# Attention: turning the spread reciprocal weights with TensorE's transpose instruction instead of with products against the identity

## The chip, the cores and the metric

The kernel runs on one core of a Trainium2 chip. The metric is the device time of one execution in microseconds, the median of several runs. Five engines work side by side and wait for each other by semaphores: TensorE (PE; its weight loads are listed apart as PEld), VectorE (DVE), ScalarE (ACT), GpSimd (POOL) and SyncE (SP), which issues most DMA.

## The reference

Four layers on `x` of 4 x 512 x 512 (batch, rows, features), each added to its input:

```python
x = x + top5120_mask(fside * cond * softmax(x) / sqrt(512))   # 1: a mask of ones, diagonal excluded
xn = rms_norm(x) * g_norm * (1 + scale(cond)) + shift(cond)    # 2: attention, 16 heads of 32
q, k, v = heads(xn @ W_qkv); q, k = rms_norm(q)*g_q, rms_norm(k)*g_k
attn = softmax(q @ k.T / sqrt(32)); o = attn @ v
x = x + o + o @ W_out
x = x + gru(x)                                                 # 3: 512 time steps, one after the other
x = x + grid_sample(x, cond)                                   # 4
```

The change concerns the division in the softmax of layer 2: each row of `attn @ v` of a head is divided by the sum of the exponentials of that row.

## The kernel before, in words

The program of every engine is written out by hand, in order, with semaphores between them. The order is: the search for the 5120th value (some 200 us), then the attention of batch 0, 1, 2 and 3 (`pe_attention`, `act_attention`, `dve_attention`), then the 512 recurrent steps (some 1,520 us).

The attention of a batch `b` has two parts. The first projects q, k and v (L1654), stacks and turns q and k (L1673) and, from the second batch on, multiplies the output of the batch before by W_out (L1696). The second runs 32 units, `UNITS`: 4 groups `g` of 4 heads, in each 4 tiles `t` of 128 queries, in each 2 pairs of heads. For unit n:

- PE makes two score tiles of 128 x 512 (`pe_scores`, L1717), two units ahead of the rest (`AHEAD`).
- DVE takes the row maxima of both (`dve_maxima`, L1279); POOL (L515; for batch 3 DVE, L1282) scales and negates them.
- ACT makes the exponentials of the two tiles and their row sums `k.weight` (`act_exponentials`, L750).
- PE transposes them, eight tiles of 128 x 128 in float32 (`pe_turn`, L1733); ACT (L795) and DVE (L1363) copy one half each out of PSUM.
- PE multiplies by v with four heads side by side in the array (`pe_weighted_values`, L1751), one quarter of half a group per unit, four units behind.

Because a group's result is held with features on partitions (`k.oT`, 128 features x 512 queries) but the sums stand with queries on partitions, the reciprocals must be turned. DVE makes the reciprocals of a group's sums (L1371) in the last unit of the group. POOL spreads each over the 32 features of its head into `k.oT[:, g]` (L471): 4 tiles of 128 queries x 128 features. `pe_divide` (L1757 to L1767) turns these four tiles into one PSUM bank: this is the place of the change. ACT copies the bank back over `k.oT[:, g]` (`act_divide`, L757), and DVE multiplies the group's products by it (`dve_divide`, L1290).

In PE's order, `pe_divide` of group g stands at the end of unit 8g + 11 for g below 3, between that unit's values (L1751) and the next unit's scores (L1717); for g = 3 it stands after the last values of the batch and before the transposes and normings for the next batch (`pe_columns`, L1619 and L1630), or in batch 3 before the products with W_out (L1696). There are 16 calls, four tiles each. In ACT's and DVE's order the two steps behind it stand in unit 8g + 12: ACT's copy after the exponentials of unit 8g + 13 and before L795, DVE's product after the maxima of unit 8g + 14 and before L1363. PE waits in `pe_divide` for POOL's spread and for DVE's product of the group before.

Of the kernel before, what the change touches and what calls it, by code (L numbers as in the profile page):

```python
# [16 lines left out]
P = 128  # L17
B, S, D = 4, 512, 512
# [359 lines left out]
VALUES_BANK, DIVIDE_BANK = (6, 7, 6, 7), (7, 6, 7, 6)  # L378
# [1378 lines left out]
def pe_divide(e, k, b, g):  # L1757
    s = k.sem
    n = NC * b + g
    e.wait_ge(s["inv_spread"], n + 1)  # L1760
    if g:
        e.wait_ge(s["out_cols"], n)
    else:
        e.wait_ge(s["heads_dve"], TURNS * (b + 1))
    for t in range(NT):
        made = e.matmul(k.bank(DIVIDE_BANK[g], S)[:, t * P:(t + 1) * P], k.oT[:, g, t * P:(t + 1) * P], k.ident[:], start=True, stop=True)  # L1766
    made.then_inc(s["inv_turned"], 1)  # L1767


def pe_attention(e, k, b):  # L1770
# [26 lines left out]
    for n, (g, t, pair) in enumerate(UNITS):  # L1797
        if n + AHEAD < len(UNITS):
            pe_scores(e, k, b, n + AHEAD)
        pe_turn(e, k, b, n)  # L1800
        if n >= 4:
            group, kt = divmod(n - 4, 4)
            pe_weighted_values(e, k, b, group // 2, group % 2, kt)
            if group % 2 == 1 and kt == NT - 1:
                pe_divide(e, k, b, group // 2)
    for kt in range(NT):
        pe_weighted_values(e, k, b, NC - 1, 1, kt)
    pe_divide(e, k, b, NC - 1)
    if b + 1 < B:
        pe_columns(e, k, b + 1)  # L1810
# [159 lines left out]
```

## Time and profile before

| | |
|---|---|
| median of 3 runs | 2298.03 us (2296.3 to 2299.89) |
| the profiled execution | 2292.36 us, its span 2290.5 us |
| PE busy | 2179.2 us (95%) |
| PE weight loads busy | 1837.8 us (80%) |
| DVE busy | 1528.3 us (67%) |
| ACT busy | 1279.5 us (56%) |
| POOL busy | 485.6 us (21%) |

A busy share is a mean over stages with different limits, so it says little on what one edit is worth. The chain of waits (the work that ended last, followed back from the end) tells which engine's time the end depends on in each stretch, and the rows of a stretch in order of time tell by how much the next engine is behind.

### The profile page before, as it was taken

How to read it: one execution, taken by the hardware profiler on the slowest of the kernel's cores; microseconds unless marked ns; L12 is line 12 of the kernel's file. 1: busy time of each engine (PE TensorE's matmuls, PEld its weight loads, DVE VectorE, ACT ScalarE, POOL GpSimd, SP SyncE). 2: the span in 40 equal slices, each digit the busy share in tenths (PEclk: the TensorE clock that was granted, in tenths of full speed). 3: DMA queues.
4: the chain of work that ended last, by engine and by line, in shares of the span. 5: the costliest groups of instructions: out<-in, count | busy, mean ns of one | idle time of the engine just before them, and what ended most of it. 6: DMA issues, size and time to landing. Idle time of an engine off the chain costs nothing.

```text
span 2290.5 us, 130384 instructions
## 1 busy us (share of the span) xinstructions
PE 2179.2 (95%) x56333; PEld 1837.8 (80%) x56333; DVE 1528.3 (67%) x6093; ACT 1279.5 (56%) x5574; POOL 485.6 (21%) x2271
## 2 busy tenths in 40 slices
PE   5768999999989999999999999999999999999998
PEld 3654655645545899999999999999999999999997
DVE  7987867768677456655665565566666566666665
ACT  6765947749468355566444454454545444454444
POOL 2002121021110122232222222222222222222222
PEclk8569999999999999999999999999999999999999
DMA  5000000010010000000000000000000000000000
GB/s 204 3 2 1 1 1 1 1 56 1 1 56 1 22 4 5 5 5 5 5 5 9 5 9 4 9 10 5 9 9 5 9 5 10 10 5 14 12 9 16
DMA packets 8711, 31.49 MB, mean 14 GB/s; under 512 B 1028, under 2 KB 1352, under 8 KB 7880
## 3 DMA queue, kind: packets, MB, share of 16 engines
q1 hardware_dynamic: 7712, 23.07, 2.7%
q8 instruction: 444, 7.27, 1.3%
q14 instruction: 131, 1.07, 0.1%
q10 hardware_dynamic: 424, 0.07, 0.0%
HBM read 18.94 MB, written 4.19 MB: 10 GB/s over the span
## 4 chain that ended last, share of the span: by engine, by line
PE 82%; DVE 11%; ACT 3%; issue 2%; DMA 1%; POOL 0%; SPq 0%; DVEq 0%; POOLq 0%; ACTq 0%
PE psum L1923 53%; PE psum L1830 9%; PE psum L1733 4%; PE psum L1654 3%; PE psum L1751 3%; PE psum L1696 2%; PE psum L1717 2%; PE psum L1857 2%; DVE region_cols L1102 2%; DVE region_cols L1086 2%; DVE top L1279 1%; PE psum L1673 1%; DMA region_cols<-in_L_cond_W_emb_dram 1%; PE psum L1766 1%; PE psum L1870 1%
## 5 line engine op out<-in xcount | busy, mean ns | idle before, releaser
L563 POOL TENSOR_TENSOR region_w_b<-region_w_b 128x16 f32<-128x16 f32 x1022 | 223.2, 218 | 1153.1 <-DVE region_w_b L1488 1153.1
L1923 PE MATMUL psum<-parts1A,region_w_hh 128*128 128x40 f16 x12288 | 429.6, 179 | 2.9 <-issue 1.1
L1923 PE MATMUL psum<-parts0A,region_w_hh 128*128 128x40 f16 x12288 | 428.9, 179 | 3.1 <-ACT psum L819 0.9
L1923 PE MATMUL psum<-parts1B,region_w_hh 128*128 128x40 f16 x12288 | 428.9, 179 | 1.1 <-issue 0.5
L1923 PE MATMUL psum<-parts0B,region_w_hh 128*128 128x40 f16 x12288 | 428.4, 179 | 1.1 <-issue 0.9
L1923 PEld LDWEIGHTS psum<-parts1A,region_w_hh 128*128 128x128 f16 x12288 | 381.1, 96 | 41.0 <-DVE parts1A L1497 5.7
L1923 PEld LDWEIGHTS psum<-parts0A,region_w_hh 128*128 128x128 f16 x12288 | 380.9, 96 | 40.2 <-DVE parts0A L1497 4.4
L915 ACT ACTIVATE mixA<-rzA 128x8 f32<-128x8 f32 x512 | 110.8, 216 | 535.1 <-DVE rzA L1462 535.1
L1923 PEld LDWEIGHTS psum<-parts1B,region_w_hh 128*128 128x128 f16 x12288 | 363.3, 96 | 3.3 <-issue 1.6
L1923 PEld LDWEIGHTS psum<-parts0B,region_w_hh 128*128 128x128 f16 x12288 | 362.9, 95 | 3.0 <-issue 1.5
L1462 DVE TENSOR_REDUCE rzA<-psum 128x8 f32<-128x32 f32 x512 | 98.2, 192 | 278.9 <-PE psum L1923 278.4
L1830 PE MATMUL psum<-region_cols,region_w_a 128*128 128x256 f32 (+1 forms) x864 | 252.5, 389 | 0.9 <-DVE region_cols L1268 0.9
L1488 DVE TENSOR_TENSOR_SCAN region_w_b<-giveB,region_w_b 128x40 f32<-128x40 f32 x512 | 123.8, 242 | 145.2 <-ACT region_w_b L929 145.2
L565 POOL COPY region_work<-region_w_b 128x8 f32<-128x8 f32 x1024 | 207.2, 202 | 2.3 <-DVE region_w_b L1488 2.3
L750 ACT ACTIVATE region_rows<-psum,neg_top 128x512 f32<-128x512 f32 x256 | 174.2, 687 | 33.8 <-POOL neg_top L515 21.6
L1488 DVE TENSOR_TENSOR_SCAN region_w_b<-giveA,region_w_b 128x40 f32<-128x40 f32 x512 | 123.6, 241 | 95.2 <-ACT region_w_b L929 95.1
L1279 DVE TENSOR_REDUCE top<-psum 128x2 f32<-128x1024 f32 x128 | 156.0, 1220 | 29.1 <-PE psum L1717 29.0
L1654 PE MATMUL psum<-region_w_a,region_work 128*128 128x512 f32 x384 | 174.1, 607 | 0.0
L922 ACT ACTIVATE giveB<-rzB 128x8 f32<-128x8 f32 x512 | 110.9, 217 | 99.1 <-DVE rzB L1469 98.6
L1733 PEld LDWEIGHTS psum<-ident,region_rows 128*128 128x128 f32 x1024 | 118.9, 142 | 40.1 <-issue 17.6
L1733 PE MATMUL psum<-ident,region_rows 128*128 128x128 f32 x1024 | 139.0, 276 | 7.7 <-ACT region_work L795 4.1
L929 ACT ACTIVATE region_w_b<-nlineB 128x8 f32<-128x8 f32 x512 | 111.4, 218 | 58.7 <-DVE nlineB L1477 8.9
(243 smaller groups left out, 3303.1 us busy)
## 6 DMA issues: line engine op xcount, KB each, us to landing
region_rows<-in_x_dram SPq DMA_DIRECT2D x4, 1024.0 KB, 11.2
region_w_a<-in_L_cond_W_qkv_dram SPq DMA_DIRECT2D x1, 3072.0 KB, 23.2
region_w_hh<-in_L_cond_W_hh_dram SPq DMA_DIRECT2D x4, 768.0 KB, 6.6
region_w_a<-in_L_cond_W_ih_dram SPq DMA_DIRECT2D x1, 3072.0 KB, 10.2
out_dram<-region_w_b SPq DMA_DIRECT2D x12, 256.0 KB, 2.3
region_cond<-in_cond_dram SPq DMA_DIRECT2D x2, 1024.0 KB, 7.8
region_cols<-in_L_cond_W_emb_dram SPq DMA_DIRECT2D x1, 2048.0 KB, 19.7
region_w_out<-in_L_cond_W_out_dram SPq DMA_DIRECT2D x1, 1024.0 KB, 21.5
```

Source lines behind the costliest of these rows:

```text
L563: e.tensor_tensor(k.line[half][:, :, :, 1:3], new.unsqueeze(3).broadcast_to([P, 2, B, 2]), k.signs.unsqueeze(1).unsqueeze(1).broadcast_to( ...
L565: e.tensor_copy(k.state[:, st + 1, 2 * half:2 * half + 2], new).then_inc(s[f"kept{h}"], 1)
L750: e.activation(k.probs[b][:, 2 * pair + i], k.bank(2 * pair + i, S), ACT.Exp, scale=logit_scale, bias=k.neg_top[:, col + i:col + i + 1], a ...
L915: e.activation(k.mix[half][:, :, :, 3], k.rz[half][:, 0], ACT.Sigmoid, scale=unscale).then_inc(s[f"rsig{h}"], 1)
L922: e.activation(k.give[half][:, :, :, 2], k.rz[half][:, 1], ACT.Sigmoid, scale=minus_unscale).then_inc(s[f"give{h}"], 1)
L929: e.activation(k.line[half][:, :, :, 0], k.nline[half][:, :, :, 3], ACT.Tanh, scale=unscale).then_inc(s[f"tanh{h}"], 1)
L1279: e.tensor_reduce(k.top[:, cols], k.psum[:, 2 * pair:2 * pair + 2], AX.X, ALU.max).then_inc(s["top"], 1)
L1488: e.tensor_tensor_scan(k.spread[half].rearrange("p c b q -> p (c b q)")[:, 0::2], k.give[half][:].rearrange("p c b q -> p (c b q)"), k.lin ...
L1654: made = e.matmul(k.bank(bank, D), k.xnT[:, c, t * P:(t + 1) * P], k.w_qkv[:, c, i * D:(i + 1) * D], start=(c == 0), stop=(c == NC - 1))
L1733: made = e.transpose(k.bank(bank, NT, P)[:, kt], k.probs[b][:, slot, kt * P:(kt + 1) * P], k.ident[:])
L1830: made = e.matmul(k.bank(SIDE_BANK[number % 2], B * LENGTHS[q]), k.w_ih[:, c, block * P:(block + 1) * P], k.xT[:, c, :, STARTS[q]:STARTS[q ...
L1923: made = e.matmul(k.slots(bank)[:, :, ch, :, 0:2], k.w16[:, 2 * read + c, part, NC * "rzn".index(g) + 2 * half + ch], k.parts[now][read][: ...
```

## The change

`pe_divide` issues a transpose of each tile against the identity in place of a matrix product of the tile with the identity. Operands, bank, order and semaphores stay as they are; `e.transpose` is the call that `pe_turn` makes.

```diff
     for t in range(NT):
-        made = e.matmul(k.bank(DIVIDE_BANK[g], S)[:, t * P:(t + 1) * P], k.oT[:, g, t * P:(t + 1) * P], k.ident[:], start=True, stop=True)
+        made = e.transpose(k.bank(DIVIDE_BANK[g], S)[:, t * P:(t + 1) * P], k.oT[:, g, t * P:(t + 1) * P], k.ident[:])
     made.then_inc(s["inv_turned"], 1)
```

## Rows read from the trace of the kernel before

**Rows 1.** Busy time by stretch: PE, PEld, DVE, ACT, POOL, granted clock, DMA.

```profile
250.24:267.44 17.20, 17.01 (x157) 10.60 (x153) 15.23 (x19) 16.01 (x42) 2.18 (x10) 1.00 0.00 1
224.00:230.00 6.00, 5.58 (x21) 4.18 (x22) 3.55 (x5) 4.95 (x14) 0.59 (x3) 0.50 0.00 0
630.00:636.00 6.00, 4.92 (x20) 3.14 (x21) 3.39 (x5) 3.85 (x6) 2.35 (x2) 0.50 0.00 0
```

**Rows 2.** Line 1766 and line 1733 (pe_turn): count, duration ns min/median/max, start us.

```profile
L1766 PE MATMUL psum<-ident,region_cond x128: 275/275/377, 250.2 to 740.3; 128*128 128x128 f32 x128
...
L1733 PE MATMUL psum<-ident,region_rows x1024: 272/273/421, 225.4 to 736.5; 128*128 128x128 f32 x171
```

**Rows 3.** The chain that ended last, 225 to 780 us: start us, us, what.

```profile
242.92 0.87 PE psum L1733 x8
...
244.90 0.87 PE psum L1733 x8
...
250.31 1.09 PE psum L1766 x8
...
296.07 1.09 PE psum L1766 x8
297.16 0.87 PE psum L1619 x8
...
739.53 1.09 PE psum L1766 x8
740.62 13.75 PE psum L1696 x32
```

**Rows 4.** PE in order of time: start us, us, engine, line, operation, count, idle before.

```profile
250.24 1.16 PE L1766 MATMUL psum<-ident,region_cond 128*128 128x128 f32 x8
251.23 0.59 PE L1717 MATMUL psum<-region_w_b,region_scratch 128*128 128x512 f16 x2
...
254.43 0.63 PE L1733 MATMUL psum<-ident,region_rows 128*128 128x128 f32 x4 [0.19 <-DVE region_work L1363]
254.99 0.64 PE L1751 MATMUL psum<-region_work,region_w_b 128*32 128x256 f32 x8
```

**Rows 5.** All engines in order of time behind the first divide.

```profile
251.78 0.59 ACT L757 ACTIVATE region_cond<-psum 128x512 f32<-128x512 f32 x1
251.86 1.23 DVE L1279 TENSOR_REDUCE top<-psum 128x2 f32<-128x1024 f32 x1 [1.14 <-PE psum L1717]
...
253.00 0.68 DVE L1290 TENSOR_TENSOR region_cond<-psum,region_cond 128x512 f32<-128x512 f32 x1
253.17 0.20 POOL L515 TENSOR_TENSOR neg_top<-top,minus_logit_scale 128x2 f32<-128x2 f32 x1 [2.77 <-DVE top L1279]
...
253.40 0.69 ACT L750 ACTIVATE region_rows<-psum,neg_top 128x512 f32<-128x512 f32 x1 [0.50 <-POOL neg_top L515]
...
255.72 0.69 ACT L750 ACTIVATE region_rows<-psum,neg_top 128x512 f32<-128x512 f32 x1 [0.39 <-POOL neg_top L515]
```

**Rows 6.** ACT's waits from 250.24 to 267.44: total us, times, longest us.

```profile
ACT region_rows L750 <- POOL neg_top L515: 0.9, 2, 0.5
```

**Rows 7.** The same in batch 3, in order of time.

```profile
694.69 1.23 DVE L1279 TENSOR_REDUCE top<-psum 128x2 f32<-128x1024 f32 x1 [0.94 <-PE psum L1717]
...
696.15 0.69 ACT L750 ACTIVATE region_rows<-psum,neg_top 128x512 f32<-128x512 f32 x1 [0.42 <-DVE neg_top L1282]
...
698.68 0.69 ACT L750 ACTIVATE region_rows<-psum,neg_top 128x512 f32<-128x512 f32 x1 [0.60 <-DVE neg_top L1282]
```

**Rows 8.** PE in order of time, early in batch 0.

```profile
225.43 1.91 PE L1733 MATMUL psum<-ident,region_rows 128*128 128x128 f32 x8
...
227.99 1.91 PE L1733 MATMUL psum<-ident,region_rows 128*128 128x128 f32 x8
```

**Rows 9.** ACT and DVE behind the last divide of batch 0.

```profile
297.20 0.60 ACT L757 ACTIVATE region_cond<-psum 128x512 f32<-128x512 f32 x1 [3.74 <-PE psum L1766]
...
297.90 0.69 DVE L1290 TENSOR_TENSOR region_cond<-psum,region_cond 128x512 f32<-128x512 f32 x1 [3.75 <-ACT region_cond L757]
```

## The prediction
> **What bounds the kernel now.** I first looked at the chain of waits through the attention stages, to see whether the changed line is on it at all. It is, every time: the line of `pe_divide`, L1766, appears 16 times with 1.09 us each, from 250.31 to 739.53 us [rows 3], 16 x 1.09 = 17.4 us of the chain. Next I looked at one line alone: the 16 calls with four tiles each show as 128 products, so a float32 product with the identity runs as two passes; `pe_turn`, 4 batches x 32 units x 8 tiles = 1,024 tiles, shows 1,024 [rows 2], one pass per tile. Their durations are the same (275 and 273 ns), so what counts is the number of instructions and their distance, not the duration of one. Then I looked at a whole group period, from one divide to the next: 17.20 us, in which PE is busy 17.01, ACT 16.01 and DVE 15.23 us, at a granted clock of 1.00 [rows 1]. That is the reader's warning: PE is only just ahead of ACT, and a saving on PE arrives only as far as ACT still has idle time in the period. ACT has 0.9 us of it, in two waits, both for the negated maxima and both right behind the divide [rows 6]. In the other units of the period ACT has no listed wait, so there ACT sets the rhythm.
>
> **The price of one divide, before and after.** The burst of eight L1766 starts at 250.24 and the scores behind it at 251.23 [rows 4]: 0.99 us from start to start. For four transposes with work on either side there is a row too: four L1733 start at 254.43 and the values behind them at 254.99, 0.56 us [rows 4]. That burst began after an idle of 0.19 us, as the divide's burst begins with its first weight load open. So the first estimate of the saving is 0.99 - 0.56 = 0.43 us. From the other side: eight L1733 in a stream take 0.87 us of the chain, 0.109 each [rows 3], so four take 0.435, and if the whole of the divide's 1.09 us on the chain shrank to that, 0.65 us would go. Halving the burst with its fixed start kept gives a value between: 0.99 less four passes of 0.109 to 0.12 is 0.51 to 0.55 left, 0.44 to 0.48 saved. I take 0.45 us, near the row of a real four-burst, and keep 0.43 and 0.65 as ends.
>
> **What of it arrives, mid-batch (12 of 16).** After the first divide the chain goes: scores end 0.45 us earlier; DVE, which sat idle 1.14 us for them [rows 5], starts the maxima at 251.41 instead of 251.86. They end by 252.55 (the next DVE step starts 1.14 behind their start). DVE's product L1290 needs ACT's copy L757, which is bound to ACT's own order and not to PE: it starts at 251.78 as before, and where the product waits for that copy alone it starts 0.70 behind the copy's start (297.20 and 297.90) [rows 9], so it is free from 252.48, 0.07 us before it is needed. L1290 can so start at 252.55, 0.45 earlier. With the value of 0.65 it would be held at 252.48, so 0.52 us is the ceiling for these divides. The negated maxima come 0.45 us earlier: ACT's exponentials start at 252.95 instead of 253.40, just when the copy L795 lets ACT go (253.40 less the idle 0.50 is 252.90). So the first wait, 0.50, shrinks to 0.05. The second wait, 0.39 before 255.72 [rows 5], hangs on DVE's queue (product, copy L1363, next maxima), which is 0.45 earlier, as ACT is: it remains about 0.39. The sum of ACT's waits falls from 0.9 to 0.45 per period, and all else in the period is back to back; the period becomes 17.20 - 0.45 = 16.75 us, with ACT at 16.01. For 9 divides of batches 0 to 2: 9 x 0.45 = 4.05 us.
>
> In batch 3 DVE negates the maxima itself. DVE's idle before the maxima is 0.94 us and ACT's two waits are 0.42 and 0.60 [rows 7]. The first vanishes (0.42 of 0.45), and the second, at DVE's pace, takes the remaining 0.03: 0.45 again, 3 x 0.45 = 1.35 us.
>
> **What arrives at the ends of batches (4 of 16).** Here nothing runs beside PE that could be late: PE goes from the divide (1.09 us at 296.07) straight into the next batch's transposes at 297.16 [rows 3]; ACT sat idle 3.74 us for the divide [rows 9]. In batch 3 the W_out products follow without a gap, 13.75 us from 740.62 [rows 3]. All of 0.45 arrives, 4 x 0.45 = 1.80 us.
>
> **Moved or added.** Nothing is moved; no semaphore and no DMA is added, and POOL's spread, which the divide waits for, is made four units earlier mid-batch. The transfers of W_hh, W_ih and the grid start some microseconds earlier with what releases them. The recurrent stage of 1,520 us is behind all this and is unchanged in its instructions.
>
> **Sum.** 4.05 + 1.35 + 1.80 = 7.20 us. The profiled execution took 2292.36 us (span 2290.5 plus 1.9 around it) and would take 2285.2. The median of the runs shown is 5.7 us above the profiled one; nothing makes the saving depend on that, so from 2298.03 it gives 2290.8 us, 0.31% less.
>
> **A rule of the Trainium skill weighed against the rows.** Transposes in `pe_turn` run at a granted clock of 1.00 in the group's period, where eight of them per unit are the largest part of PE's work [rows 1, 3]. The Trainium skill (TensorE: Matmul & The Clock Gate, Part 4: PE-mode transpose) speaks against the change: it gives about 275 ns for a transpose inside a kernel, and says that the full clock does not engage for transposes because they do not count as PE work in the same way. Its duration agrees with the 273 ns here; taken as the price of each transpose it would make an estimate of 1.10 us for four, more than today's 0.99. By that the fourth rival would hold, by its rule on the clock the third.
>
> **The rivals.**
> First, the whole of the chain's difference goes: 0.65 us where no other engine holds, so 0.52 x 9 + 0.65 x 3 + 0.65 x 4 = 9.2 us, 2288.8. For it: the chain counts 1.09 us, and the loads may be better hidden with four. Against it: the four-burst of [rows 4]. Chance 0.12.
> Second, mid-batch nothing arrives, because some tie between ACT and DVE that I take for slack is none; only the four ends count: 1.8 us, 2296.2. For it: ACT is at 16.01 of 17.20. Against it: ACT's two waits directly behind the divide, and 1.14 us of idle DVE. Chance 0.07.
> Third, slower: with the 128 passes of products gone and transposes in their place, PE counts as less active and the clock falls more often in the unit loop. It does fall in this kernel: the granted clock is 0.50 from 224 to 230 us and again from 630 to 636 [rows 1], both outside these group periods. Price: at the low level the bursts of L1733 are 2.56 us apart (225.43 to 227.99) [rows 8], against 1.98 us at the full one (242.92 to 244.90) [rows 3], so a fall over some 6 us costs (6/2.56) x 0.58 = 1.4 us. It turns the sign from the sixth fall on (7.2/1.4); with one in each of the 12 periods it would cost 16.8, net 9.6 slower, 2307.6. Against it: PE has no gap in these periods, and transposes already carry them. Chance 0.04.
> Fourth, the change does not do what it says: the transpose of this operand runs as two passes too (nothing changes, 2298.0), or transposes do not overlap and each takes its 273 ns, 4 x 0.273 = 1.09 us against 0.99, 16 x 0.10 = 1.6 us slower, 2299.6. Against it: 1,024 single passes on the same types and shapes [rows 2], 0.109 us apart. Chance 0.02.
>
> **How the numbers follow.** My forecast has 0.75; its own range, with 0.40 to 0.50 per divide (6.4 to 8.0) and a spread of the runs of 1.8 us to either side of the median, is 2288 to 2293. About 0.2%, 4.6 us, is what a measurement of this kernel tells from no change. The forecast and the first rival are beyond that unless the measurement errs by 2.6 us: nearly all of 0.87. The second and fourth are within it. Something left over that this change could shift by chance, such as the fall near 630 us or a tenth of a percent in the recurrent stage (1.5 us), makes up the rest. That gives 0.86 faster, 0.11 same, 0.03 slower. The range goes from 2286.5 (the first rival with some noise) to 2295.5, short of the second rival.
>
> **What would show it right or wrong.** L1766 with 64 instructions and about 0.55 us to the next start; mid-batch periods of 16.75 us; ACT's first wait behind the divide near 0.05 and the second still near 0.4; the start of the recurrent steps 7.2 us earlier, and their length unchanged. It is wrong if the burst takes more than 0.75 us, if ACT's second wait grows by what the first one loses, or if the clock falls inside a period.

## The result, and the profile after

The changed kernel takes 2288.09 us (median of 7 runs, 2283.74 to 2293.69) against 2298.03 (7 runs, 2296.05 to 2300.36), ratio 0.9967 with a 95% interval of 0.9955 to 0.9979: 7.6 us less (4.8 to 10.3). The two medians alone differ by 9.9 us; the recorded ratio is an estimate of its own, and it is the one with an interval. A second timing of the same kernel gave 0.9957 (0.9942 to 0.9971). The profiled execution took 2289.45 us, its span 2287.7.

The changed line in the trace after (count, duration ns min/median/max, start us) answers to [rows 2]:

```profile
L1766 PE MATMUL psum<-ident,region_cond x64: 272/273/330, 250.7 to 734.7; 128*128 128x128 f32 x64
```

64 instructions in place of 128, one per tile. From the start of the first divide to the start of the work behind the last one it is 484.1 us, against 490.2 before: 6.1 us less. The savings as they show in single periods and ends (0.46 to 0.51 each) add up to 7.8 us; where the rest went stands below. One group period, from divide to divide, in the view of busy time by stretch [rows 1]:

```profile
250.67:267.38 16.71, 16.39 (x152) 10.14 (x148) 15.28 (x19) 15.98 (x42) 2.19 (x10) 1.00 0.00 1
```

17.20 us have become 16.71. PE's busy time falls by 0.62 in it, ACT's and DVE's are unchanged, and the granted clock is 1.00 as before. All engines in order of time behind the first divide, which starts at 250.67 here and at 250.24 in [rows 4, 5]:

```profile
250.67 0.66 PE L1766 MATMUL psum<-ident,region_cond 128*128 128x128 f32 x4
...
251.16 0.59 PE L1717 MATMUL psum<-region_w_b,region_scratch 128*128 128x512 f16 x2
...
251.80 1.22 DVE L1279 TENSOR_REDUCE top<-psum 128x2 f32<-128x1024 f32 x1 [0.64 <-PE psum L1717]
...
252.22 0.59 ACT L757 ACTIVATE region_cond<-psum 128x512 f32<-128x512 f32 x1
252.69 0.60 ACT L795 ACTIVATE region_work<-psum 128x512 f32<-128x512 f32 x1
...
252.94 0.68 DVE L1290 TENSOR_TENSOR region_cond<-psum,region_cond 128x512 f32<-128x512 f32 x1
252.95 0.64 PE L1751 MATMUL psum<-region_work,region_w_b 128*32 128x256 f32 x8 [0.32 <-ACT region_cond L757]
...
253.33 0.69 ACT L750 ACTIVATE region_rows<-psum,neg_top 128x512 f32<-128x512 f32 x1
...
255.70 0.69 ACT L750 ACTIVATE region_rows<-psum,neg_top 128x512 f32<-128x512 f32 x1 [0.44 <-POOL neg_top L515]
```

From the divide's start to the scores behind it there are now 0.49 us (250.67 to 251.16), 0.99 before. DVE's wait for the scores falls from 1.14 to 0.64. ACT's wait of 0.50 before its exponentials is gone, the next one of 0.39 has become 0.44. DVE's product L1290 starts 0.72 us behind ACT's copy L757 and 1.14 us behind the start of DVE's own maxima, so its two limits, 0.70 [rows 9] and 1.14 [rows 5], now meet. One thing is late where it was not: PE itself waits 0.32 us before L1751 for ACT's copy. The chain of waits shows the change of owner. At the first two divides of batches 0 to 2 it no longer goes through L1766, but through ACT (start us, us, what):

```profile
251.46 0.86 ACT region_rows L750 x3
252.32 0.50 ACT region_cond L757
252.82 0.14 issue
252.95 0.64 PE psum L1751 x8
```

At a batch's third divide and at its end the divide is still on the chain, 0.59 us instead of the 1.09 of [rows 3]:

```profile
295.07 0.59 PE psum L1766 x4
295.66 0.87 PE psum L1619 x8
```

**Where 7.8 us became 6.1.** The distance from the last divide of batch 2 to the first of batch 3 grew from 106.0 to 107.2 us although one saving of 0.5 lies in it: 1.7 us are lost there. It is the projection of batch 3. PE in order of time, before and after:

```profile
631.08 1.89 PE L1673 MATMUL psum<-ident,region_work 128*128 128x128 f16 x16 [4.51 <-DVE region_work L1251]
632.76 5.54 PE L1654 MATMUL psum<-region_w_a,region_work 128*128 128x512 f32 x8
...
648.38 1.07 PE L1673 MATMUL psum<-ident,region_work 128*128 128x128 f16 x16 [2.27 <-DVE region_work L1251]
649.29 3.65 PE L1696 MATMUL psum<-region_cond,region_w_out 128*128 128x512 f32 x8
```

```profile
625.74 1.89 PE L1673 MATMUL psum<-ident,region_work 128*128 128x128 f16 x16 [4.51 <-DVE region_work L1251]
627.42 5.03 PE L1654 MATMUL psum<-region_w_a,region_work 128*128 128x512 f32 x8
...
643.05 1.20 PE L1673 MATMUL psum<-ident,region_work 128*128 128x128 f16 x16 [2.78 <-DVE region_work L1251]
644.04 5.25 PE L1696 MATMUL psum<-region_cond,region_w_out 128*128 128x512 f32 x8
```

Before, one of PE's two waits for DVE is followed by slow work (1.89 us where 1.07 is usual); after, both are (5.25 where 3.65 is usual). The granted clock in these stretches of after (us, PE busy, clock, DMA):

```profile
624.00:630.00 6.00, 4.26 (x19) 0.50 0.00 0
644.00:647.00 3.00, 3.00 (x7) 0.50 1.01 422
```

0.50 is the lower of the clock's two levels, 1.2 GHz. The divides do not stand in this stretch. The two waits are linked: behind the first one the eight products took 5.54 us before and 5.03 after, so after PE came 0.5 us sooner to the second wait, which DVE ends, and stood there 2.78 us instead of 2.27.

**The rest of the span.** The first and last start of the 512 recurrent steps, before and after:

```profile
L1462 DVE TENSOR_REDUCE rzA<-psum x512: 180/192/193, 768.2 to 2280.0; 128x8 f32<-128x32 f32 x171
```

```profile
L1462 DVE TENSOR_REDUCE rzA<-psum x512: 180/192/194, 762.6 to 2277.2; 128x8 f32<-128x32 f32 x171
```

The steps start 5.6 us earlier (the first divide started 0.4 later than before), but take 1514.6 us instead of 1511.8. So this pair of profiles differs by only 2.8 us of span (2290.5 to 2287.7), and the medians by 9.9. How much of that is chance can only be told from more executions.

### The profile page after: what moved, and what is told of

The parts are those of the page before. It is cut to its first block, busy times and chain, and to the rows that moved or that the text cites. A ratio compares the mean times of both kernels' runs of the same rounds, so it can differ in the third digit from the quotient of the medians.

```text
span 2287.7 us, 130256 instructions
## 1 busy us (share of the span) xinstructions
PE 2174.7 (95%) x56269; PEld 1832.3 (80%) x56269; DVE 1531.9 (67%) x6093; ACT 1279.5 (56%) x5574; POOL 486.7 (21%) x2271
## 3 DMA queue, kind: packets, MB, share of 16 engines
q14 instruction: 131, 1.07, 0.2%
## 4 chain that ended last, share of the span: by engine, by line
PE 81%; DVE 12%; ACT 4%; issue 2%; DMA 1%; POOL 0%; SPq 0%; POOLq 0%; ACTq 0%; DVEq 0%
PE psum L1923 53%; PE psum L1830 9%; PE psum L1733 3%; PE psum L1654 3%; PE psum L1696 2%; PE psum L1751 2%; PE psum L1857 2%; PE psum L1717 2%; DVE region_cols L1102 2%; DVE region_cols L1086 2%; DVE top L1279 2%; ACT region_rows L750 1%; PE psum L1673 1%; DMA region_cols<-in_L_cond_W_emb_dram 1%; PE psum L1870 1%
## 5 line engine op out<-in xcount | busy, mean ns | idle before, releaser
L1477 DVE TENSOR_TENSOR_SCAN nlineA<-mixA,psum 128x32 f32<-128x32 f32 x512 | 113.1, 221 | 43.6 <-PE psum L1923 1.4
## 6 DMA issues: line engine op xcount, KB each, us to landing
region_w_a<-in_L_cond_W_ih_dram SPq DMA_DIRECT2D x1, 3072.0 KB, 10.3
```

The costliest lines, as they stand in the source:

```text
L1477: e.tensor_tensor_scan(k.nline[half][:].rearrange("p c b q -> p (c b q)"), k.mix[half][:].rearrange("p c b q -> p (c b q)"), k.bank(N_BANK ...
```

## The experiments

All times are medians; a ratio is to the kernel before on the same chip, and again the recorded estimate, not the quotient of two medians.

**The changed kernel once more.** No edit.

> The changed kernel once more, as the yardstick of the other runs. Theory: the attention's part of the change is fixed (mid-batch period 16.71 us, 10.91 us from the third divide to the fourth), and what differs between executions lies in the recurrent stage (first to last step 1511.8 us in the profile of before, 1514.6 in that of after) and in falls of the clock in batch 3's projection. So the periods again within 0.02 us, the recurrent stage anywhere within 3 us of 1514, and a ratio to the kernel before of 0.996 to 0.998. Rival: the change itself lengthens the recurrent stage by some 3 us, and it is again above 1514.

2286.41 us, ratio 0.9957 (0.9942 to 0.9971). Periods of 16.70 us; 106.9 us before batch 3, again two falls of the clock; recurrent steps 1513.5 us. The attention repeats to 0.01 us per period, the recurrent stage does not.

**Code length restored.**

```diff
+    for _ in range(NC * NT * B):
+        e.transpose(k.bank(6, P), k.ident[:], k.ident[:])
     e.wait_ge(s["w_emb_in"], 16)
```

> The changed kernel with 64 transposes of the identity into an unused bank added near the start, where PE waits 14.7 us for W_emb, so that PE's program has the length of the kernel before from there on. Theory that the place of PE's code matters for the recurrent stage: it takes the 1511.8 us of before again, and executions spread by 4 us as before and not by 10. Rival, chance from execution to execution: no such return, time as the changed kernel's within 2 us. Both expect mid-batch periods of 16.71 us, and nothing for the 64 transposes (7 us inside the 14.7 of idle).

2287.38 us, ratio 0.9963 (0.9950 to 0.9975). Recurrent steps 1513.0 us. In the eleven profiles of kernels of this study that leave no work out, all with the same recurrent program, that stage took between 1511.4 and 1516.3 us: 1511.8 before, 1514.6 and 1513.5 for the changed kernel, 1513.0 with the padding, 1511.9, 1514.5 and 1515.4 for the next three below, 1511.4 and 1516.3 for the two with moved steps, 1514.6 and 1514.4 for the two with filled waits. The highest and lowest belong to kernels whose PE program is equally long. The place of PE's code does not explain it, and neither does the divide; what does was not settled. The kernel before itself spread over 10.8 us (2288.06 to 2298.85, 17 runs) in this comparison, so its narrow spread of 4.3 us in the first timing says nothing.

The 64 added transposes cost nothing where they stand (the products behind PE's wait for W_emb start at 23.45 us, 23.60 in the run before), but they show something of the clock. PE had run one product in the 8.5 us before them. PE in order of time, in two views:

```profile
8.55 2.96 PE L1531 MATMUL psum<-ident 128*128 128x128 f32 x13
```

```profile
11.11 5.96 PE L1531 MATMUL psum<-ident 128*128 128x128 f32 x52
```

The first 13 start 0.21 us apart, as do those of [rows 8] at a granted clock of 0.50; from 11.32 us on they start 0.11 us apart, as at 1.00. So the clock rose with nothing but float32 transposes running.

**Every tile turned twice.**

```diff
-    for t in range(NT):
+    for t in [*range(NT), *range(NT)]:
         made = e.transpose(...)
```

> Every tile of the divide is transposed twice (the same result written again), so the divide has eight single passes again. Theory that only PE's time in the burst counts: burst 0.93 us to the next start (0.49 plus 4 x 0.109), period 16.71 + 0.44 = 17.15 us, batch ends 0.44 longer, total 16 x 0.44 = 7.0 us above the changed kernel, 1 us below the kernel before. Rival: the gain comes from the kind of instruction (its loads, its place beside the fp16 scores) and not from the number; then the time stays within 2 us of the changed kernel.

2293.24 us, ratio 0.9992 (0.9981 to 1.0004). The divide in order of time (start us, us):

```profile
249.52 1.09 PE L1766 MATMUL psum<-ident,region_cond 128*128 128x128 f32 x8
250.45 0.59 PE L1717 MATMUL psum<-region_w_b,region_scratch 128*128 128x512 f16 x2
```

0.93 us from start to start, periods of 17.14 us (17.15 expected), 106.0 us before batch 3. The median is 6.8 us above the changed kernel's 2286.41 and 1.8 below the kernel before, 2295.05. So 0.44 of the 0.50 us per burst is PE's time for four instructions; the other 0.06 is what eight products take more than eight transposes (0.99 against 0.93).

**Mid-batch divides alone, and end-of-batch divides alone.**

```diff
+        if g < NC - 1:     # first kernel; g == NC - 1 in the second
             made = e.transpose(...)
+        else:
+            made = e.matmul(..., start=True, stop=True)
```

> Transposes for groups 0 to 2 only; the last group of each batch keeps the products. Theory: 12 of the 16 savings, periods 16.71 us, from the third divide to the fourth 10.91 as in the changed kernel (the fourth divide's own burst lies behind its start), the fourth burst again 0.99 us; 12 x 0.49 = 5.9 us below before. Rival (mid-batch nothing arrives in the end because ACT or DVE take it back): no more than 1 us below before.

2287.8 us, ratio 0.9963 (0.9948 to 0.9977). Periods 16.70, 10.91 us to the fourth divide, 99.7 us from it to the next batch's first, as before. The 48 transposes are these (count, duration, starts):

```profile
L1767 PE MATMUL psum<-ident,region_cond x48: 272/273/329, 249.2 to 722.0; 128*128 128x128 f32 x48
```

> Transposes for the last group of each batch only. Theory: periods 17.20 us as before, bursts of 0.49 us at the four ends, 4 x 0.50 = 2.0 us below before, within 2 us of what can be told from no change. Rival: the next batch's columns or ACT's copy take the saving back, 0 us.

2295.08 us, ratio 1.0005 (0.9993 to 1.0018): not different from no change, 2 us not excluded. Its trace has the savings (99.25 us instead of 99.73 from a batch's fourth divide to the next one's first), and it too has the second fall of the clock: 107.1 us before batch 3 instead of 106.0. So here the fall takes 1.5 of the 2.0 us back. The timed gain of the change is in the main the mid-batch part, with 12 of the 16 savings; what the ends bring is seen in the trace, and is too small for the timing.

**One tile instead of four.**

```diff
-    for t in range(NT):
+    for t in range(1):
         made = e.transpose(...)
```

> Only the first of the four tiles is turned per divide; the other three columns of the bank are left as they are. This tells where further savings on PE would go. Ceiling theory: mid-batch DVE's product is held by ACT's copy L757 (0.70 behind its start), and PE's values for the next group are held by the same copy (PE idle 0.32 us before L1751 in the changed kernel), so a burst 0.33 us shorter brings less than 0.05 per period: 16.67 to 16.71 us; at the four ends all of it arrives, 0.33 less each. Rival, no ceiling: periods of 16.4 us.

2288.38 us (one run, beside 2293.64 of the kernel before). In order of time behind a divide:

```profile
250.65 1.23 DVE L1279 TENSOR_REDUCE top<-psum 128x2 f32<-128x1024 f32 x1 [0.31 <-PE psum L1717]
...
252.09 0.69 DVE L1290 TENSOR_TENSOR region_cond<-psum,region_cond 128x512 f32<-128x512 f32 x1 [0.21 <-ACT region_cond L757]
...
252.13 0.64 PE L1751 MATMUL psum<-region_work,region_w_b 128*32 128x256 f32 x8 [0.64 <-ACT region_cond L757]
```

Periods 16.71 us: of 0.33 us more saved on PE nothing arrives in batches 0 to 2. What DVE wins on the scores (0.33) it waits for L757 (0.21), and PE's wait before L1751 doubles from 0.32 to 0.64. From the fourth divide on to the next batch the whole 0.33 arrives (98.92 instead of 99.26). In batch 3, where L757 comes earlier against DVE's queue, the period did fall, from 16.95 to 16.67. The ceiling is shown. The prediction had put it at 0.52 us by way of DVE's product; with the copy L757 in its place it lies at 0.49, and the change uses all of it.

**Seven of eight transposes of the exponentials.**

```diff
-        for kt in range(NT):
+        for kt in range(NT - 1 if i == 0 and n >= 4 else NT):
```

> From the fifth unit of each batch on, seven instead of eight tiles of exponentials are transposed (the eighth keeps older values): 0.109 us less on PE per unit, ACT and DVE as they are. Theory of the prediction, ACT sets the rhythm in the plain units: they stay 1.98 us apart. Rival, PE sets it (the chain of waits names PE there): 1.87 us apart.

2285.83 us (one run). PE in plain units, in order of time:

```profile
255.43 0.60 PE L1717 MATMUL psum<-region_w_b,region_scratch 128*128 128x512 f16 x2
...
257.32 0.61 PE L1717 MATMUL psum<-region_w_b,region_scratch 128*128 128x512 f16 x2
...
259.27 0.61 PE L1717 MATMUL psum<-region_w_b,region_scratch 128*128 128x512 f16 x2
...
261.14 0.60 PE L1717 MATMUL psum<-region_w_b,region_scratch 128*128 128x512 f16 x2
```

The units are 1.89, 1.95 and 1.87 us apart instead of 1.98, 1.90 on average, where the theory said 1.98 and the rival 1.87. PE set the rhythm in the plain units of batches 0 to 2. ACT followed so closely that none of its waits was long enough to be listed. The period fell to 16.25 us, 0.46 of the 0.87 taken off: by then the chain of waits of these units goes through ACT's exponentials and copies, so ACT was less than 0.1 us per unit behind.

**ACT's copy earlier, and DVE's product later too.**

```diff
 act_exponentials:
+        if i and n % 8 == 5 and n > 5:
+            act_divide(e, k, b, g - 1)
 act_attention:
-        if n > 4 and n % 8 == 4:
-            act_divide(e, k, b, g - 1)
 dve_attention (second kernel only):
-        if n > 4 and n % 8 == 4:
+        if n > 5 and n % 8 == 5:
             dve_divide(e, k, b, g - 1)
```

> Only ACT's copy L757 is moved one exponential earlier; DVE's product stays where it is. Theory: PE's wait of 0.32 us before the next group's values (held by L757) goes, but DVE's queue of maxima, product, copy, maxima (1.14 + 0.60 + 0.60) still holds the second maxima, so the period stays 16.70 us. Rival: L757 alone was the ceiling, and the period falls by up to 0.3 us.

2284.42 us (one run). Periods 16.70 us as expected; PE's wait before L1751 is gone. In order of time:

```profile
251.31 0.64 PE L1751 MATMUL psum<-region_work,region_w_b 128*32 128x256 f32 x8
...
251.68 0.68 DVE L1290 TENSOR_TENSOR region_cond<-psum,region_cond 128x512 f32<-128x512 f32 x1
...
252.28 0.68 DVE L1363 COPY region_work<-psum 128x512 f32<-128x512 f32 x1
...
252.88 1.21 DVE L1279 TENSOR_REDUCE top<-psum 128x2 f32<-128x1024 f32 x1
```

DVE goes from step to step without a wait. The chain of waits is the one of the kernel before again, through the divide and DVE's product and copy (start us, us, what):

```profile
249.48 0.59 PE psum L1766 x4
...
251.68 0.68 DVE region_cond L1290
```

So behind ACT's copy stands a second limit at the same height: the old path, shorter by the 0.50 us of the burst. On this path a still shorter burst might bring more; no run shows it.

> The changed kernel with ACT's copy of the turned weights (L757) moved one exponential earlier, between the two of the unit before, and DVE's product (L1290) moved behind the maxima of the next unit. Theory: L757 holds PE's values by 0.32 us and DVE's queue by its product of 0.60 us before the next maxima; with both moved ACT's wait of 0.44 us behind the divide shrinks by 0.3, period about 16.4 us, 12 x 0.3 = 3.6 us less than the changed kernel. Rival: what L1290 delays later is again on the path (DVE is busy 15.2 of 16.7 us), and the period stays 16.7.

2287.14 us, ratio 0.9973 (0.9963 to 0.9984). The period stays at 16.70: the rival was right, the product delays a copy L1363 one unit later, and PE waits 0.19 us for that one. Only the stretch from the third to the fourth divide became shorter, by 0.28 us (0.16 in batch 3).

**Waits of the projection filled.**

```diff
 pe_turn_stack:
+    if b == B - 1 and t in (1, 2) and i == 0:
+        e.wait_ge(s["heads_act"], n)
+        for _ in range((0, 32, 16)[t]):
+            e.transpose(k.bank(6, P), k.ident[:], k.ident[:])
     e.wait_ge(s["stack_low"], 2 * n + 2)
```

> The changed kernel with 32 and 16 transposes of the identity put into PE's two waits of batch 3's projection (4.5 and 2.8 us long, for DVE's stacks), into a bank that is free there. Theory: the clock falls behind these two waits (0.50 from 624 to 630 and from 644 to 647 us) because PE stood idle; with the waits filled it stays at 1.00, the products behind them take 3.65 us for eight instead of 5.03 and 5.25, and the stretch from the last divide of batch 2 to the first of batch 3 falls from 107.2 to about 105.0 us. Rival 1: the falls come whatever PE does there, and the stretch stays at 107 us or grows by the added work. Rival 2: DVE, not PE, ends the waits, and only part of the 3 us of slower products was on the path: 106 us.

2287.18 us, ratio 0.9965 (0.9950 to 0.9980), and the stretch before batch 3 did not get shorter but took 108.1 us. Half of the theory held. PE in order of time:

```profile
617.94 3.66 PE L1666 MATMUL psum<-ident 128*128 128x128 f32 x32
622.64 1.07 PE L1677 MATMUL psum<-ident,region_work 128*128 128x128 f16 x16 [1.04 <-DVE region_work L1251]
...
634.85 1.91 PE L1666 MATMUL psum<-ident 128*128 128x128 f32 x16
639.54 1.89 PE L1677 MATMUL psum<-ident,region_work 128*128 128x128 f16 x16 [2.78 <-DVE region_work L1251]
641.22 5.83 PE L1700 MATMUL psum<-region_cond,region_w_out 128*128 128x512 f32 x8
```

Behind the first wait, now 1.04 us, the work is at full speed (1.07 us). But the next work that DVE releases came only 0.4 us sooner, 16.90 us behind the first (622.64 to 639.54) instead of 17.31 (625.74 to 643.05): PE reached the second wait sooner and stood there 4.7 us, as the second rival has it. The 16 transposes left 2.78 of it open, and the fall came there, longer than in the changed kernel. So the first fall costs 0.4 us of the stretch and the second about 1.7. The fall of the kernel before from 224 to 230 us [rows 1] is missing in this profile (granted clock 1.00 there), though the program up to there is the changed kernel's, which has it: falls also differ by chance from execution to execution.

> Both moves of ACT's copy and DVE's product and the filled waits together, as the version that might beat both kernels. Expected by addition: 12 periods as the changed kernel's, the four stretches from the third to the fourth divide 0.28 shorter (1.0 us), the stretch before batch 3 2.2 us shorter: some 3 us less than the changed kernel, ratio to the kernel before 0.995 to 0.996. Rival: nothing beyond the changed kernel, 0.9965.

2283.98 us (5 runs, 2282.20 to 2286.03), ratio 0.9957 (0.9942 to 0.9973). The same place:

```profile
641.09 1.07 PE L1677 MATMUL psum<-ident,region_work 128*128 128x128 f16 x16 [2.77 <-DVE region_work L1251]
641.99 3.65 PE L1700 MATMUL psum<-region_cond,region_w_out 128*128 128x512 f32 x8
```

No fall, with the same open wait, and 105.1 us before batch 3 against 107.2 in the kernel without the filling: 2.1 us. PE busy, granted clock and DMA from 644 to 647 us, without and with the moved steps:

```profile
644.00:647.00 3.00, 3.00 (x8) 0.73 0.10 41
```

```profile
644.00:647.00 3.00, 3.00 (x22) 1.00 0.65 270
```

The slow work is the one at the lower clock, and not the one with more transfers beside it. What decides whether the second wait is followed by a fall is open. In the eleven profiles without filled waits its length goes with it: 2.17 to 2.32 us in five, with no fall behind it (the kernel before, every tile twice, mid-batch alone, one tile, seven of eight), and 2.78 to 3.21 us in six, with one (both of the changed kernel, the padding, ends alone, and the two with moved steps). But of the two filled ones 2.78 was followed by a fall and 2.77 was not. This version has the lowest median of all, but its interval overlaps the changed kernel's.

## Why the prediction was right, and where not

- **The price of a divide** was forecast at 0.45 us saved and measured at 0.50 (0.99 to 0.49). The row that I went by, four transposes behind a wait of 0.19 us, counts 0.56 to the next start; without a wait ahead the burst needs 0.49. The upper end, 0.65, would have needed the start of the burst to vanish as well.
- **Mid-batch** the forecast period was 16.75 us; it is 16.71. The first of ACT's waits went (forecast 0.05 left, none is listed), the second stayed (0.44, forecast 0.39), and nothing else was in the way, though by chance of sizes: the saving just reached the ceiling, 0.49 us where 0.52 was forecast. From the third divide to the fourth 0.46 arrived.
- **"There ACT sets the rhythm"** was wrong for the plain units: PE does, as the chain said. It did not matter for the forecast, because both readings give the same period as long as only the divide shrinks. A wait too short to be listed is not the same as an engine that sets the pace.
- **Missed:** PE's own wait for ACT's copy before the next group's values (they share a PSUM bank with the turned weights). I had followed L757 to DVE only.
- **Batch 3** and **the ends** came as forecast: 17.45 to 16.95 us, and 0.45 to 0.5 per end.
- **The clock** did not fall inside a period, so the third rival fell where I had put it. But it fell once more in the projection of batch 3, in the stretch that I had named only as chance. That cost 1.7 us of the 7.8 and was there in both profiles of the changed kernel. It is not the transposes as such: with every tile transposed twice, and with seven of eight exponentials, all divides are transposes and there is one fall, as in the kernel before. Whether the change makes the second fall more frequent is not shown, for the kernel before has one profile here. The price of a fall, 1.4 us in the prediction, came out as 0.4 and 1.7: the first one is largely hidden behind a wait for DVE. The Trainium skill (TensorE: Matmul & The Clock Gate, Part 4: PE-mode transpose) says that transposes do not count as PE work for the clock in the same way. These runs speak against it for float32 transposes: in the run with the padding the clock rose with nothing else running, and 32 of them put into the first wait of 4.51 us kept the clock at 1.00 behind it, in both runs that had them.
- **The sum**, 7.2 us, meets 7.6 measured (4.8 to 10.3; 9.9 by the medians, 2288.09 where 2290.8 was forecast), partly by two errors against each other: 0.6 too little for the bursts, and a loss of 1.7 not foreseen. That the time came so close is partly luck: the recurrent steps were to start 7.2 us earlier and keep their length; they started 5.6 earlier in the profile, and their length varies by 4.9 us from run to run, which is most of the forecast gain. The first rival (9.2) is not excluded by the timing, but by the bursts. The second (1.8 us) and the fourth (none, or slower) are.

## What to carry to other kernels

Count the instructions of the trace, not their durations: a float32 product with the identity and a transpose last the same 0.27 us there, but one tile takes two of the former and one of the latter, 0.11 us apart. For a saving on an engine that is only just ahead, follow every reader of what it hands on, PE itself among them; their slack is the ceiling, and here the ceiling happened to be as high as the saving (0.49 us). A saving of a third of a per cent cannot be read from one pair of profiles: here a stage that was not touched moved by up to 4.9 us, over half of the change. And before a slow stretch is blamed for its whole length, look at who ends the next wait: a fall of the clock that slowed PE by 2.2 us (1.89 + 5.03 us of work where 1.07 + 3.65 is usual) cost 0.4, since DVE ended the wait behind it.

## What the runs showed of the hardware

- Four float32 transposes of 128 x 128 behind a running stream take 0.49 us to the next instruction's start, eight take 0.93 and eight products 0.99.
- PE's wait of 4.51 us for DVE was followed by a clock of 0.50 in all eleven profiles where it stood open; with 1.04 us of it left it was not, in two. Eight float32 products that take 3.65 us at full clock took 5.25 and 5.83 behind a fall.
- 64 float32 transposes of 128 x 128 behind an idle PE start 0.21 us apart for the first 13 and 0.11 us apart from then on: the clock rises with transposes alone.
- 512 identical recurrent steps took between 1511.4 and 1516.3 us in eleven executions, without a difference in the recurrent stage's own program.
